# Three score banks and three side banks in twelve attention passes, with some additions on VectorE

## The chip, the cores and the metric

One core of one Trainium2 chip runs the whole kernel. The metric is the device time of one execution in microseconds (us). TensorE is called PE in the rows of the profile, VectorE DVE, ScalarE ACT, GpSimd POOL, and SyncE, which issues the DMAs here, SP.

## What is computed

The reference takes 1250 tokens of width 512 and does three things to them: a mean over neighbours in a graph with two linear layers, a linear attention, and then a block with two routed experts, a cross attention and an MLP. The part that matters here is the last block's attention, done three times with 8 heads of 64 features (spatial expert, temporal expert, cross attention):

```python
def _temporal_experts(xt, idx, qw, qb, kw, kb, vw, vb, pw, pb):
    q, k, v = ...                      # linear layers of xt, (B, T, H, HD)
    logits = jnp.einsum('bthd,bshd->bhts', q, k) * HD ** (-0.5)
    causal = jnp.tril(jnp.ones((T, T), dtype=bool))
    logits = jnp.where(causal, logits, -jnp.inf)
    att = jax.nn.softmax(logits, axis=-1)
    o = jnp.einsum('bhts,bshd->bthd', att, v).reshape(B, T, D)
    o = jnp.einsum('btd,bod->bto', o, pw[idx]) + pb[idx][:, None, :]
    return xt + o
```

The spatial one and the cross attention are the same without the causal mask. Products run in float32, most of them as three products of rounded parts (hi and lo).

## The kernel before

**Passes, units, steps.** The three attentions are 12 passes of two heads each: n = 0 to 3 spatial, 4 to 7 temporal with the causal mask, 8 to 11 cross. "The eighth pass" is n = 7 and "the last" is n = 11. A pass has five units, each 250 query tokens (i = 0 to 4), and a unit has five blocks of 250 keys (b), or i + 1 blocks where the mask is on. A step g is one head of one block; there are 520, so 260 pairs of steps. `STEP[g]` is (n, i, b, h).

**What a step does.** PE computes the scores of 250 keys and 250 queries into one bank of PSUM (`score`, L2357 to L2361; a bank holds 512 float32 in each partition, and there are eight). ACT takes the exponential of the bank into a ring of eight tiles, `p_raw` (`exponent`, L1380). For each pair of steps POOL adds the two heads' exponentials into `p_sum` (`add_pair`, L1085 to L1090: one instruction of 500 columns for a unit's first block, two for each later one). PE multiplies the exponentials by the values (`product`, L2376, a block of two pairs at a time), and at the end of a unit it multiplies `p_sum` by ones, which gives the denominators (`denominator`, L2386). DVE takes the reciprocal and multiplies (`unit_out`, L1817 and L1819).

**Side work.** Between the steps PE prepares what comes later, at most three side tasks a step (`SIDE[g]`): linear layers for keys, queries and values (K, Q, V: L2260), score products from which DVE takes the largest score of each query (M: `maximum`, L2318 on PE, L1801 on DVE), the turn of these maxima into a row (R: L2329 on PE, `row_in`, L1352 on ACT), the turn of the values (T: L2339) and the weights' product for the cross attention (F: L2299). A K leaves its bank when ACT has rounded it (`key_hi`, L1297) and DVE has taken the rest (`key_lo`, L1772); a Q likewise (`query_hi` L1325, `query_lo` L1783). `key_copy` (L1305) then copies each head's keys to the other half of the partitions, in two instructions of ACT.

**Banks.** Scores use banks 0 and 1 in turn (`g % 2`), the sums of a unit banks 2 and 3 (`unit % 2`), and side work the banks from `SIDE_BANKS_AT` = 4 on. `bank_plan` walks PE's list of work and gives each side task the side bank that was taken longest ago (one held by a K, Q or F of the same step is left out); `BEFORE[entry]` is what held the bank, and PE waits for that to be read (`left`). So with two score banks the scores of step g + 2 wait for the exponential of step g.

**Order.** All engines run a list that is written out in Python. On PE, slot g is: the scores of step g + 2 (`LEAD` = 2), `SIDE[g]`, then, at every second pair, denominators and products. On ACT, slot g is: the exponential of g + 2, the copies of `SIDE[g - 1]`, then the first readings of `SIDE[g]`. On DVE: `key_lo` and `query_lo` of `SIDE[g - 1]`, the maxima of `SIDE[g]`, `unit_out`; in the last five slots of the last pass also ten normalizations of `tok_z` (L1893), two a slot. On POOL: the pair's additions, then splits of weights (L952, L954) and of the finished attention planes (L1044, L1046). Between n = 7 and n = 8 PE projects the temporal result (`project`, L2397), and after n = 11 the cross result (`proj`, L2443); both need the last unit's output.

## Time and profile before

| | |
|---|---|
| median of 3 runs | 1836.44 us (1834.28 to 1839.62) |
| the profiled execution's own time | 1838.64 us |
| its span from first to last instruction | 1836.6 us |
| PE busy | 1652.5 us (90%) |
| DVE busy | 1066.6 us (58%) |
| ACT busy | 711.8 us (39%) |
| POOL busy | 875.5 us (48%) |
| attention steps, first to last score | about 467 to 1545 us |

The terms of a sum are made on the profiled execution. PE is the engine to follow: between the ends of the graph part and of the attention it is hardly ever idle, and all other engines feed it or read from it. Matmuls are pipelined and overlap in the rows, so the distance from start to start tells more than the busy time: a product of 250 columns starts 0.12 us after the one before it when nothing is in its way.

### The profile page before, as it was taken

What the parts mean: (1) busy time and instruction counts of PE and PEld (TensorE: products, weight loads), DVE (VectorE), ACT (ScalarE), POOL (GpSimd) and SP (SyncE); (2) the same over time, 40 slices, a digit from 0 to 9 for tenths busy, and PEclk for the clock granted to TensorE, in tenths of its full rate; (3) what the DMA queues carried; (4) which work ended last, traced back from release to release, by engine and by line L of the source; (5) the groups of instructions that cost most, each with busy time, mean ns of one, the idle gap of its engine ahead of it and who ended that gap; (6) DMA issues with size and microseconds to landing.
All of it is one profiled execution on the core that took longest, in us unless ns stands there. A gap on an engine that the chain in (4) does not pass through costs nothing. (4 is left out here: it accounts for less than half of the span.)

```text
span 1836.6 us, 32041 instructions
## 1 busy us (share of the span) xinstructions
PE 1652.5 (90%) x10735; PEld 1378.3 (75%) x10735; DVE 1066.6 (58%) x2221; ACT 711.8 (39%) x1346; POOL 875.5 (48%) x815
## 2 busy tenths in 40 slices
PE   2899988876899999999999997899999996899998
PEld 1788757755777888778878876788788874797896
DVE  7778768885556445654564562665555555683332
ACT  1223211114666445556555552464546553120010
POOL 3213001102587657684644466156566689383440
PEclk9999999988999999999999998899999998999999
DMA  3101000011031100030000000000000002121111
GB/s 116 35 7 47 12 1 29 18 49 50 12 125 41 35 19 7 1 130 12 18 13 7 7 1 24 17 19 7 7 13 13 1 1 85 40 74 35 46 35 56
DMA packets 24788, 58.06 MB, mean 32 GB/s; under 512 B 2537, under 2 KB 4805, under 8 KB 24013
## 3 DMA queue, kind: packets, MB, share of 16 engines
q1 hardware_dynamic: 24650, 56.18, 9.5%
q8 instruction: 92, 1.51, 0.3%
q14 instruction: 46, 0.38, 0.1%
HBM read 44.87 MB, written 11.30 MB: 31 GB/s over the span
## 5 line engine op out<-in xcount | busy, mean ns | idle before, releaser
L1801 DVE TENSOR_REDUCE max_part<-ps 125x2 f32<-125x500 f32 x520 | 328.1, 674 | 224.9 <-PE ps L2318 199.9
L1380 ACT ACTIVATE p_raw<-ps 125x500 f32<-125x500 f32 x520 | 296.9, 586 | 280.7 <-PE ps L2361 271.8
L1088 POOL TENSOR_TENSOR p_sum<-p_sum,p_raw 125x500 f32<-125x500 f32 x200 | 232.5, 1163 | 222.9 <-ACT p_raw L1380 215.7
L2376 PE MATMUL ps<-p_raw,v_rows 125*64 125x250 f32 x2080 | 248.5, 380 | 0.0
L1090 POOL TENSOR_TENSOR p_sum<-p_sum,p_raw 125x500 f32<-125x500 f32 x200 | 232.5, 1163 | 15.7
L2376 PEld LDWEIGHTS ps<-p_raw,v_rows 125*64 125x64 f32 x2080 | 143.4, 137 | 73.5 <-issue 4.5
L1641 DVE TENSOR_SCALAR onehot<-iota_h,win_key,key_t 125x320 f16 x453 | 176.9, 390 | 0.5 <-issue 0.4
L1817 DVE RECIPROCAL feat<-ps 128x250 f32<-128x250 f32 x60 | 103.0, 1717 | 113.8 <-PE ps L2386 113.6
L2260 PE MATMUL ps<-xa_hi,w_hi 128*128 128x418 f32 (+1 forms) x448 | 150.1, 335 | 14.5 <-POOL w_lo L954 9.1
L2357 PE MATMUL ps<-q_both_a,k_both_a 128*125 128x250 f32 x520 | 154.3, 317 | 9.4 <-ACT p_raw L1380 7.6
L2318 PE MATMUL ps<-k_both_a,q_both_a 128*125 128x250 f32 x520 | 143.8, 292 | 20.6 <-issue 9.1
L1640 DVE TENSOR_SCALAR onehot<-iota_h,low_t 125x125 f16 x453 | 128.2, 283 | 47.4 <-issue 26.5
L2357 PE MATMUL ps<-q_both_b,k_both_b 128*125 128x250 f32 x520 | 141.9, 294 | 12.9 <-ACT p_raw L1380 12.8
L2260 PE MATMUL ps<-xa_lo,w_hi 128*128 128x418 f32 (+1 forms) x448 | 148.3, 331 | 0.0
L2260 PE MATMUL ps<-xa_hi,w_lo 128*128 128x418 f32 (+1 forms) x448 | 148.0, 330 | 0.0
L2357 PEld LDWEIGHTS ps<-q_both_a,k_both_a 128*125 128x125 f32 x520 | 98.2, 189 | 65.5 <-issue 50.2
L2318 PE MATMUL ps<-k_both_b,q_both_b 128*125 128x250 f32 x520 | 140.5, 285 | 0.0
L2361 PE MATMUL ps<-q_row_a,k_rest_a 65*125 65x250 f32 x520 | 139.3, 289 | 0.0
L2361 PE MATMUL ps<-q_row_b,k_rest_b 128*125 128x250 f32 x520 | 137.8, 287 | 0.0
L2318 PEld LDWEIGHTS ps<-k_both_a,q_both_a 128*125 128x125 f32 x520 | 97.5, 188 | 27.7 <-issue 11.3
L952 POOL CAST w_hi<-w_raw 128x512 fp32r<-128x512 f32 x44 | 28.4, 645 | 183.4 <-PE ps L2361 48.2
L2357 PEld LDWEIGHTS ps<-q_both_b,k_both_b 128*125 128x125 f32 x520 | 98.2, 189 | 18.9 <-ACT p_raw L1380 18.6
(395 smaller groups left out, 3723.0 us busy)
## 6 DMA issues: line engine op xcount, KB each, us to landing
w_raw<-in_w_mlp SPq DMA_DIRECT2D x32, 256.0 KB, 2.7
w_raw<-in_w_gps SPq DMA_DIRECT2D x16, 256.0 KB, 2.6
w_raw<-in_w_tp SPq DMA_DIRECT2D x16, 256.0 KB, 2.6
w_raw<-in_w_sp SPq DMA_DIRECT2D x12, 256.0 KB, 2.7
w_raw<-in_w_cr SPq DMA_DIRECT2D x12, 256.0 KB, 2.6
d_xt<-xb_hi SPq DMA_DIRECT2D x1, 2508.0 KB, 9.4
d_xt<-xb_lo SPq DMA_DIRECT2D x1, 2508.0 KB, 15.0
xa_hi<-d_xt SPq DMA_DIRECT2D x1, 2508.0 KB, 9.3
```

The source lines that it names most:

```text
L1088: pool.tensor_tensor(total, total, halves[0], ALU.add).then_inc(s_add, 1)
L1090: pool.tensor_tensor(total, total, halves[1], ALU.add).then_inc(s_add, 1)
L1380: act.activation(p_raw[:, g % PR, :], ps[0:TOK, g % 2, 0:4 * TOK], ACT.Exp, scale=SCALE).then_inc(s_exp, 1)
L1640: dve.tensor_scalar(row[:, 0:ET], iota_h[0:ET, 0:ET], low, None, ALU.is_equal)
L1641: ins = dve.tensor_scalar(row[:, ET:ET + DH], iota_h[0:ET, :], win_key[0:ET, bass.ds(w, 1)], key, ALU.add, ALU.is_equal)
L1801: dve.tensor_reduce(part[:, y, :, j], ps[0:TOK, bank, 0:4 * TOK].rearrange("p (h k) -> p h k", h=2), AX.X, ALU.max)\
L1817: dve.reciprocal(out, ps[:, 2 + u % 2, 2 * TOK:4 * TOK]).then_inc(s_share, 1)
L2260: ins = pe.matmul(ps[:, bank, 0:width], w[:, ROLE_SLOT[role], 128 * c:128 * c + 128], x[:, c, first:first + width], start=(c == 0 and y == ...
L2318: ins = pe.matmul(to, q_both[h][:, ring(n, i), tile], k_both[h][:, n % 2, keys], start=True, stop=not masked)
L2357: pe.matmul(to, k_both[h][:, n % 2, tile], q_both[h][:, ring(n, i), :], start=True, stop=False)
L2361: ins = pe.matmul(to, k_rest[h][rest, n % 2, tile], q_row[h][rest, ring(n, i), :], start=False, stop=True)
L2376: ins = pe.matmul(ps[r, bank, 0:2 * TOK], v_rows[:, n % 2, kt, h, :], p_raw[:, (g - 1 + h) % PR, cols], start=(b == 0 and x == 0), stop=last)
```

## The change

Scores get three banks, 0 to 2 (`g % SCORE_BANKS`), the sums of a unit move to banks 3 and 4 (`OUT_BANK`), and side work keeps banks 5 to 7. In passes 7 and 11 (`SHARED`) POOL adds only the first head of each pair, in instructions of 250 columns, and DVE adds the second (`add_second_head`), at the head of its slot and behind a wait for that step's exponential; a semaphore of its own, `s_add_b`, tells PE's denominators and ACT's ring of these. `key_copy` is split: one head's copy in the slot after the K, as before, the other's one slot later (`third_out`), so the semaphore counts to six a pass.

```diff
-SIDE_BANKS_AT = 4
+SCORE_BANKS = 3
+OUT_BANK = 3
+SIDE_BANKS_AT = 5
...
+SHARED = (7, 11)
+SHARED_NO = {(n, i, b): 2 * x + 2 - (5 * y + i + 1) for y, n in enumerate(SHARED) for x, (m, i, b) in
+             [(x, at) for x, at in enumerate(at for at in ADDED if at[0] in SHARED) if at[0] == n]}
...
         if kind == "S":
-            use = [entry[1] % 2]
+            use = [entry[1] % SCORE_BANKS]
...
-            use = [2 + unit_of(entry[1]) % 2] if STEP[entry[1]][2] == 0 else []
+            use = [OUT_BANK + unit_of(entry[1]) % 2] if STEP[entry[1]][2] == 0 else []
...
-                total = p_sum[:, u % 2, :, :]
-                halves = [p_raw[:, (g - 1) % PR:(g - 1) % PR + 2, 2 * TOK * x:2 * TOK * (x + 1)] for x in range(2)]
-                pool.wait_ge(s_exp, g + 1)
+                heads = 1 if n in SHARED else 2
+                total = p_sum[:, u % 2, 0:heads, :]
+                halves = [p_raw[:, (g - 1) % PR:(g - 1) % PR + heads, 2 * TOK * x:2 * TOK * (x + 1)] for x in range(2)]
+                pool.wait_ge(s_exp, g - 1 + heads)
...
-                for h, r in enumerate(HALF):
-                    ins = act.activation(k_both[h][HALF[1 - h], n % 2, cols], f32(k_both[h][r, n % 2, cols]), ACT.Copy)
-                ins.then_inc(s_k_both, 1)
+                act.activation(k_both[h][HALF[1 - h], n % 2, cols], f32(k_both[h][HALF[h], n % 2, cols]), ACT.Copy).then_inc(s_k_both, 1)
...
                     act.wait_ge(s_add, ADD_NO[n, i, b])
+                    if n in SHARED:
+                        act.wait_ge(s_add_b, SHARED_NO[n, i, b])
...
+                    if g > first + 1:
+                        for task in SIDE[g - 2]:
+                            third_out(task)
...
+            def add_second_head(g):
+
+                n, i, b, _ = STEP[g]
+                u, done = 5 * n + i, SHARED_NO[n, i, b]
+                total = p_sum[:, u % 2, 1, :]
+                halves = [p_raw[:, g % PR, 2 * TOK * x:2 * TOK * (x + 1)] for x in range(2)]
+                dve.wait_ge(s_exp, g + 1)
+                if b == 0:
+                    dve.wait_ge(s_den, u - 1)
+                    dve.tensor_tensor(total, halves[0], halves[1], ALU.add).then_inc(s_add_b, 1)
+                else:
+                    dve.wait_ge(s_add_b, done - 2)
+                    dve.tensor_tensor(total, total, halves[0], ALU.add).then_inc(s_add_b, 1)
+                    dve.wait_ge(s_add_b, done - 1)
+                    dve.tensor_tensor(total, total, halves[1], ALU.add).then_inc(s_add_b, 1)
...
                 for g in range(first, end):
+                    if STEP[g][0] in SHARED and STEP[g][3] == 1:
+                        add_second_head(g)
...
-                pe.wait_ge(s_k_both, 3 * n + 3)
+                pe.wait_ge(s_k_both, 6 * n + 6)
...
                 pe.wait_ge(s_add, ADD_NO[n, i, blocks_in(n, i) - 1])
+                if n in SHARED:
+                    pe.wait_ge(s_add_b, SHARED_NO[n, i, blocks_in(n, i) - 1])
```

PE's instructions keep their order; what changes is what they wait for. In pass 5, at slot 232, stand the turned maxima of unit 2 (L2329), two score products for the maxima of unit 3 (L2318), the scores of step 235 (L2357), and in slot 233 the queries of unit 4 (L2260). Before:

```order
5535 L2329 MATMUL ps<-ident,max_col 33x125 [waits s_max_col,s_max_part]
5536 L2329 MATMUL ps<-ident,max_col 33x125
5537 L2318 MATMUL ps<-k_both_a,q_both_a 125x250 [waits s_k_both,s_q_lo,s_max_part]
5538 L2318 MATMUL ps<-k_both_b,q_both_b 125x250
5539 L2318 MATMUL ps<-k_both_a,q_both_a 125x250 [waits s_k_both,s_q_lo,s_max_part]
5540 L2320 MATMUL ps<-causal_mask,identb 125x250
5541 L2318 MATMUL ps<-k_both_b,q_both_b 125x250
...
5549 L2260 MATMUL ps<-xa_hi,w_hi 128x250 [waits s_w_split,s_k_lo]
```

The same place of the changed kernel, where the line numbers are 34 higher:

```order
5535 L2363 MATMUL ps<-ident,max_col 33x125 [waits s_max_col,s_max_part]
5536 L2363 MATMUL ps<-ident,max_col 33x125
5537 L2352 MATMUL ps<-k_both_a,q_both_a 125x250 [waits s_k_both,s_q_lo,s_max_part]
5538 L2352 MATMUL ps<-k_both_b,q_both_b 125x250
5539 L2352 MATMUL ps<-k_both_a,q_both_a 125x250 [waits s_k_both,s_q_lo,s_k_lo]
5540 L2354 MATMUL ps<-causal_mask,identb 125x250
5541 L2352 MATMUL ps<-k_both_b,q_both_b 125x250
...
5549 L2294 MATMUL ps<-xa_hi,w_hi 128x250 [waits s_w_split,s_max_in]
```

The wait for DVE's rest of the keys (`s_k_lo`) has moved from the Q in row 5549 to the second maximum in row 5539, two side tasks earlier, and the Q now waits for ACT's reading of the row that was turned in row 5535 (`s_max_in`).

ACT in the same slots: the readings of the K of pass 6 (L1297), the copies (L1305), the maxima's row (L1352), exponentials (L1380) and the first reading of the Q (L1325). Before:

```order
580 L1380 ACTIVATE p_raw<-ps 125x500
581 L1297 ACTIVATE k_both_a<-ps,tp_vecs 64x418
582 L1297 ACTIVATE k_both_b<-ps,tp_vecs 64x418
583 L1380 ACTIVATE p_raw<-ps 125x500
584 L1305 ACTIVATE k_both_a<-k_both_a 64x418
585 L1305 ACTIVATE k_both_b<-k_both_b 64x418
586 L1352 ACTIVATE q_row_a<-ps 1x250
587 L1352 ACTIVATE q_row_b<-ps 1x250
588 L1380 ACTIVATE p_raw<-ps 125x500
589 L1325 ACTIVATE q_both_a<-ps,tp_vecs 64x250
```

The changed kernel:

```order
587 L1387 ACTIVATE p_raw<-ps 125x500
588 L1304 ACTIVATE k_both_a<-ps,tp_vecs 64x418
589 L1304 ACTIVATE k_both_b<-ps,tp_vecs 64x418
590 L1387 ACTIVATE p_raw<-ps 125x500
591 L1311 ACTIVATE k_both_a<-k_both_a 64x418
592 L1357 ACTIVATE q_row_a<-ps 1x250
593 L1357 ACTIVATE q_row_b<-ps 1x250
594 L1387 ACTIVATE p_raw<-ps 125x500
595 L1311 ACTIVATE k_both_b<-k_both_b 64x418
596 L1330 ACTIVATE q_both_a<-ps,tp_vecs 64x250
```

The second copy has moved behind the row and the next exponential.

DVE at the end of the last pass, from the output of the last unit but one (L1817, L1819) to the rest of the attention planes (L1900). Before:

```order
1602 L1817 RECIPROCAL feat<-ps 128x250
1603 L1819 TENSOR_TENSOR feat<-ps,feat 128x250
1604 L1893 TENSOR_SCALAR tok_z<-tok_z,ln_mv,ln_r 125x512 x8
1605 L1817 RECIPROCAL feat<-ps 128x250
1606 L1819 TENSOR_TENSOR feat<-ps,feat 128x250
1607 L1893 TENSOR_SCALAR tok_z<-tok_z,ln_mv,ln_r 125x512 x2
1608 L1900 TENSOR_TENSOR oc_lo<-feat,oc_hi 128x418 x3
```

The changed kernel, with the unit's additions of the second head (L1838 to L1843) between them:

```order
1674 L1838 TENSOR_TENSOR p_sum<-p_raw 125x250
1675 L1841 TENSOR_TENSOR p_sum<-p_sum,p_raw 125x250
1676 L1843 TENSOR_TENSOR p_sum<-p_sum,p_raw 125x250
...
1679 L1849 RECIPROCAL feat<-ps 128x250
1680 L1851 TENSOR_TENSOR feat<-ps,feat 128x250
1681 L1927 TENSOR_SCALAR tok_z<-tok_z,ln_mv,ln_r 125x512 x4
1682 L1841 TENSOR_TENSOR p_sum<-p_sum,p_raw 125x250
1683 L1843 TENSOR_TENSOR p_sum<-p_sum,p_raw 125x250
1684 L1927 TENSOR_SCALAR tok_z<-tok_z,ln_mv,ln_r 125x512 x4
1685 L1841 TENSOR_TENSOR p_sum<-p_sum,p_raw 125x250
1686 L1843 TENSOR_TENSOR p_sum<-p_sum,p_raw 125x250
1687 L1849 RECIPROCAL feat<-ps 128x250
```

The last denominators now need additions (rows 1685 and 1686) that stand behind all eight of the first normalizations.

## Rows read from the trace of the kernel before

**Rows 1.** Waits: engine, line, what it waited for: us in total, times, longest.
```profile
PEld ps L2357 <- ACT p_raw L1380: 33.8, 62, 3.0
...
PE ps L2357 <- ACT p_raw L1380: 20.4, 46, 2.6
...
PE ps L2386 <- POOL p_sum L1090: 18.5, 3, 9.6
```
**Rows 2.** Timeline of PE, pass 9: start, us, engine, line, xcount, [idle before].
```profile
1321.18 0.44 PE L2357 MATMUL ps<-q_both_b,k_both_b 128*125 128x250 f32 x1 [1.79 <-ACT p_raw L1380]
```
**Rows 3.** Timeline of ACT at the same place.
```profile
1319.19 0.55 ACT L1305 ACTIVATE k_both_b<-k_both_b 64x418 fp32r<-64x418 f32 x1
```
**Rows 4.** Timeline of PE, pass 5: second maximum, queries, next unit's maxima.
```profile
939.95 0.28 PE L2318 MATMUL ps<-k_both_a,q_both_a 128*125 128x250 f32 x1
...
941.44 0.38 PE L2260 MATMUL ps<-xa_hi,w_hi 128*128 128x250 f32 x1 [0.20 <-DVE k_rest_b L1772]
...
943.88 0.28 PE L2318 MATMUL ps<-k_both_a,q_both_a 128*125 128x250 f32 x1
...
945.70 0.38 PE L2318 MATMUL ps<-k_both_a,q_both_a 128*125 128x250 f32 x1 [1.42 <-DVE q_both_b L1783]
```
**Rows 5.** Timeline of PE, pass 1: a maximum, two side tasks behind a turned row.
```profile
637.70 0.28 PE L2318 MATMUL ps<-k_both_a,q_both_a 128*125 128x250 f32 x1
```
**Rows 6.** Timeline of ACT at the same place: the row's reading.
```profile
637.74 0.37 ACT L1352 ACTIVATE q_row_b<-ps 1x250 fp32r<-1x250 f32 x1
```
**Rows 7.** Timeline of PE at the end of pass 7.
```profile
1127.45 1.10 PE L2386 MATMUL ps<-p_sum,ones_f 125*64 125x250 f32 x4 [9.61 <-POOL p_sum L1090]
```
**Rows 8.** Stretches: busy us and (xcount) by engine, granted clock, DMA share, GB/s.
```profile
1129.00:1133.00 4.00, 4.00 (x13) 3.81 (x12) 3.34 (x5) 1.44 (x3) 0.00 (x0) 0.50 0.00 0
1135.00:1139.00 4.00, 4.00 (x23) 3.95 (x22) 0.00 (x0) 0.00 (x0) 0.00 (x0) 1.00 0.00 0
1524.00:1529.00 5.00, 3.77 (x18) 2.18 (x20) 2.14 (x2) 0.00 (x0) 4.82 (x6) 0.50 0.32 134
```
**Rows 9.** Groups of POOL, 1088 to 1128 us: busy, mean ns | idle before.
```profile
L1088 POOL TENSOR_TENSOR p_sum<-p_sum,p_raw 125x500 f32<-125x500 f32 x9 | 10.4, 1158 | 0.3
...
L1046 POOL TENSOR_TENSOR k_rest_b<-feat,k_rest_a 128x418 fp32r<-128x418 f32 x3 | 2.8, 927 | 0.2
```
**Rows 10.** Groups of DVE, 1066 to 1098 us: the maxima.
```profile
L1801 DVE TENSOR_REDUCE max_part<-ps 125x2 f32<-125x500 f32 x24 | 15.4, 675 | 4.7 <-PE ps L2318 2.9 <-PE ps L2320 1.5
```
**Rows 11.** Groups of DVE, 1472 to 1520 us: the maxima.
```profile
L1801 DVE TENSOR_REDUCE max_part<-ps 125x2 f32<-125x500 f32 x31 | 19.8, 675 | 16.6 <-PE ps L2318 16.4
```
**Rows 12.** Timeline of PE at the end of pass 11.
```profile
1525.22 1.10 PE L2386 MATMUL ps<-p_sum,ones_f 125*64 125x250 f32 x4 [4.53 <-POOL p_sum L1090]
...
1551.43 1.10 PE L2386 MATMUL ps<-p_sum,ones_f 125*64 125x250 f32 x4 [4.36 <-POOL p_sum L1090]
1560.21 0.76 PE L2443 MATMUL ps<-wout_hi,oc_hi 128*125 128x512 f32 x1 [7.68 <-DVE oc_lo L1900]
```
**Rows 13.** Timeline of DVE, end of pass 11; last row: beside an idle POOL.
```profile
1544.23 0.42 DVE L1819 TENSOR_TENSOR feat<-ps,feat 128x250 f32<-128x250 f32 x1
1544.56 9.91 DVE L1893 TENSOR_SCALAR tok_z<-tok_z,ln_mv,ln_r 125x512 f32<-125x512 f32 x8
1554.39 1.71 DVE L1817 RECIPROCAL feat<-ps 128x250 f32<-128x250 f32 x1
...
1578.32 1.92 DVE L1942 TENSOR_SCALAR tok_z<-tok_x,end_mv,end_r 125x512 f32<-125x512 f32 x4
```
**Rows 14.** Timeline of POOL after pass 7.
```profile
1143.13 0.61 POOL L952 CAST w_hi<-w_raw 128x512 fp32r<-128x512 f32 x1 [15.73 <-PE ps L2397]
...
1145.06 1.85 POOL L952 CAST w_hi<-w_raw 128x512 fp32r<-128x512 f32 x1
```
**Rows 15.** Timeline of DVE beside the second of these.
```profile
1144.66 1.78 DVE L1830 TENSOR_TENSOR feat<-feat,xa_lo 128x1254 f32<-128x1254 f32 x1
```

More of the change, by code:

```diff
@@ L717, in build @@
         s_add = sem("s_add")
+        s_add_b = sem("s_add_b")
         s_den = sem("s_den")
@@ L1298, in key_hi, with key_copy @@
                 ins.then_inc(s_k_hi, 1)
-            def key_copy(n, p):
+            def key_copy(n, p, h):
                 cols = slice(NP * p, NP * p + NP)
                 act.wait_ge(s_k_hi, 3 * n + p + 1)
-                for h, r in enumerate(HALF):
-                    ins = act.activation(k_both[h][HALF[1 - h], n % 2, cols], f32(k_both[h][r, n % 2, cols]), ACT.Copy)
-                ins.then_inc(s_k_both, 1)
+                act.activation(k_both[h][HALF[1 - h], n % 2, cols], f32(k_both[h][HALF[h], n % 2, cols]), ACT.Copy).then_inc(s_k_both, 1)
             def query_bias(n):
@@ L1379, in exponent @@
                     act.wait_ge(s_add, ADD_NO[n, i, b])
-                act.activation(p_raw[:, g % PR, :], ps[0:TOK, g % 2, 0:4 * TOK], ACT.Exp, scale=SCALE).then_inc(s_exp, 1)
+                    if n in SHARED:
+                        act.wait_ge(s_add_b, SHARED_NO[n, i, b])
+                act.activation(p_raw[:, g % PR, :], ps[0:TOK, g % SCORE_BANKS, 0:4 * TOK], ACT.Exp, scale=SCALE).then_inc(s_exp, 1)
             def first_out(task):
@@ L1401, in second_out, with third_out @@
                 if what == "K":
-                    key_copy(*at)
+                    key_copy(*at, 0)
                 if what == "Q":
                     query_copy(*at)
+            def third_out(task):
+                what, *at = task
+                if what == "K":
+                    key_copy(*at, 1)
             act.wait_ge(s_ld_ev, 32)
@@ L1426, in _ @@
                 query_hi(n, 0)
-                key_copy(n, 0)
-                key_copy(n, 1)
-                key_copy(n, 2)
+                for p in range(3):
+                    for h in range(2):
+                        key_copy(n, p, h)
                 value_feat(n, 0)
@@ L1816, in unit_out @@
                 dve.wait_ge(s_den, u + 1)
-                dve.reciprocal(out, ps[:, 2 + u % 2, 2 * TOK:4 * TOK]).then_inc(s_share, 1)
+                dve.reciprocal(out, ps[:, OUT_BANK + u % 2, 2 * TOK:4 * TOK]).then_inc(s_share, 1)
                 dve.wait_ge(s_share, u + 1)
-                dve.tensor_tensor(out, ps[:, 2 + u % 2, 0:2 * TOK], out, ALU.mult).then_inc(s_o, 1)
+                dve.tensor_tensor(out, ps[:, OUT_BANK + u % 2, 0:2 * TOK], out, ALU.mult).then_inc(s_o, 1)
             def project(j, cols, done):
@@ L2355, in score @@
                     tile = slice((2 * b + x) * TOK, (2 * b + x + 1) * TOK)
-                    to = ps[0:TOK, g % 2, 2 * TOK * x:2 * TOK * (x + 1)]
+                    to = ps[0:TOK, g % SCORE_BANKS, 2 * TOK * x:2 * TOK * (x + 1)]
                     pe.matmul(to, k_both[h][:, n % 2, tile], q_both[h][:, ring(n, i), :], start=True, stop=False)
@@ L2366, in product @@
                 n, i, b, _ = STEP[g]
-                bank = 2 + unit_of(g) % 2
+                bank = OUT_BANK + unit_of(g) % 2
                 pe.wait_ge(s_exp, g + 1)
@@ L2382, in denominator @@
                 n, i = u // 5, u % 5
-                bank = 2 + u % 2
+                bank = OUT_BANK + u % 2
                 pe.wait_ge(s_add, ADD_NO[n, i, blocks_in(n, i) - 1])
+                if n in SHARED:
+                    pe.wait_ge(s_add_b, SHARED_NO[n, i, blocks_in(n, i) - 1])
                 for h, r in enumerate(HALF):
```

## The prediction, made before the changed kernel ran

> **What bounds the kernel now.** I read the waits of the attention first, then the timelines at the places that they name. PE is the engine to follow. Its waits there are of three kinds. Many short ones are scores that wait for an exponential [rows 1]: by the weight loads 33.8 us in 62 places, by the matmuls 20.4 us in 46. The second kind is three denominators that wait for POOL's additions, 18.5 us [rows 1]: 9.61 us at the end of the eighth pass [rows 7], 4.53 and 4.36 us at the end of the last [rows 12]. The third kind is side work that waits for DVE or ACT to read its bank or to finish an operand, as the maximum behind the queries' rest [rows 4]. So there is no single bound engine to relieve: PE would run through if three small supplies were a little earlier, and the change speeds up two of them and takes a bank from the third.
>
> **The change part by part.** All terms are for the profiled execution, 1838.64 us, which lies 2.2 us above the median of 1836.44.
>
> *Three banks for scores.* The scores of step g + 2 now need the exponential of g - 1, not of g. That exponential ends a whole step earlier, and a step with its side work is longer than nearly every wait seen: the longest is 3.0 us [rows 1]. The sample place shows why: in pass 9 scores waited 1.79 us [rows 2], because ACT stood in two key copies of 0.55 us, the second of them [rows 3], and in a row's reading before the exponential. With three banks that exponential isn't on the path of these scores. The weight loads' sum of 33.8 us overlaps work that is still running, the matmuls' sum of 20.4 us leaves out the restart; from the distances of starts in the timeline I get about 30. I take -28, with bounds of -20 and -33. The split key copy brings an exponential 0.55 us forward where a row or an exponential stands behind it, and puts the other head's copy one slot later, where its readers are at least a slot away. With three banks little is left for it to gain: 0, bounds -2 and +3.
>
> *Three banks for side work.* Now a side task waits for the reader of the task three back instead of four. I walked the new owners along the times of before. Five patterns come out. (a) The second maximum behind a K waits for the keys' rest. In pass 5 it starts at 939.95 and the rest is ready at about 941.4, when the Q started that waited for it [rows 4]: +1.5. The next maximum at 943.88 then waits for the queries' rest, which came at 945.6 [rows 4] and was waited for anyway, so a part is only moved: 1.3 net, at about 5 places, 6.5 us. (b) A maximum behind a turned row waits for its reading: in pass 1 the maximum starts at 637.70 [rows 5], the reading began at 637.74 and took 0.37 [rows 6], so about 0.4 plus a restart of 0.1, less a quarter of a microsecond of wait that it replaces: 0.26 at 22 places, 5.7 us. (c) A linear layer whose bank a query or key holds: at most the size of that wait for the queries' rest, 1.42 [rows 4], in the mean 1.07, at 8 places: 8.5 us. (d) Bursts of maxima: DVE takes 675 ns for one [rows 10], PE four products of 0.12 us, and one bank less means that the burst is felt one task earlier: 0.45 at 20 places, 9 us. (e) A few single keys and maxima, 4 us. The sum is +34. The upper bound is what all new latenesses add up to if none is absorbed by another, +69, of which half is not to be believed, since a late task makes its successors late too; I take 55. If later waits absorb most of it, 15 is left. I take 34, since I followed each pass with its shifts.
>
> *Denominators of the eighth pass.* POOL has no gap from 1088 us to the wait's end: idle before its additions is 0.3 us, an instruction of 500 columns takes 1158 ns, one of 418 columns 927 [rows 9]. By proportion 250 columns take 0.58 and by the line through both 0.45; I take 0.6, for the fixed part. That is 0.55 saved in each of some 20 instructions, 11 us, more than the 9.61 [rows 7]; the wait goes, what is next is the last exponential, so I count -9.5. Behind the wait PE's granted clock was 0.50: 13 matmuls in 4 us, 23 in 4 us when it was 1.00 again [rows 8]. From 1127.5 until 1133.6, where it changed, that lost 6.1 x (1 - 13/23), some 2.7 us. Without the idle time I count them back: -12.2 in all, bounds -4 and -13.
>
> *Denominators of the last pass.* The same relief comes to the first wait of 4.53 [rows 12], with the halved clock after it [rows 8] worth 2 us more: -6.5, bounds -3 and -7. At the last wait of 4.36 [rows 12] it is not the same. The additions of the second head stand on DVE behind normalizations that took 9.91 us for eight, 1.24 us each beside a busy POOL; beside an idle one the same form takes 0.48 [rows 13]. If POOL is half idle, eight take about 7 us; the four additions that now stand before the last denominators add 1.6 to 3. In the old order the reciprocal had to wait behind the eight anyway, until 1554.39 [rows 13]. So the end of that DVE chain, which the projection waits for (7.68 us [rows 12]), moves by little: -1.5, bounds -5 and +3. The three denominators together: **-20**, bounds -10 and -25.
>
> *VectorE's additions.* No row shows such an instruction. A product of 250 columns with an operand in PSUM took 0.42 [rows 13]; if it has to take turns with POOL's halved addition, the 0.6 of above comes on top. So 0.4 to 1.0 each. In the stretch of pass 7 that I looked at, DVE's idle time before the 24 maxima is 4.7 us [rows 10], and some 7 pairs come in, 14 additions of 0.4 or more, 5.6 us at least. That doesn't fit, so the maxima come later there and their banks with them: +3, bounds 0 and +8. In pass 11 the idle time is 16.6 us in 48 [rows 11] and some 32 additions want 13 us and up: +4, bounds 0 and +14. Each addition waits for its exponential at the slot's head, and the queries' rest and the maxima are queued behind it; this is in those bounds. Together +7.
>
> The sum: -28 + 34 - 20 + 7 = -7. 1838.6 - 7 = 1831.6, less 2.2 for the median: **1829.4**.
>
> **The rivals.** *(1) Side banks become the bound.* If a step's three side tasks do not absorb each other's lateness, the side term is 47, and with DVE short of time in the passes 7 and 11 the additions cost 9: -27 + 47 - 18 + 9 = +11, so 1847. It decides from a side term of about 45 on. For it speaks that three supplies (keys' rest, queries' rest, turned row) each show at least one wait with four banks already [rows 4]; against it that most of these are waits for an operand, which are there with any number of banks.
>
> *(2) The additions take turns.* POOL's CAST of 512 columns took 0.61 us when alone, and 1.85 us when DVE ran an addition with both inputs in SBUF [rows 14], from 1144.66 on for 1.78 us [rows 15]: it ended when DVE's did and its own 0.6 were over. If POOL's halved additions stand still while DVE's run, they take 0.6 + 0.4 = 1.0 instead of 1.16, 3 us are saved of 9.61, the clock stays low behind the rest, and the terms are -4 at pass 7, -6.5 at pass 11, and +8 for DVE: -28 + 34 - 10.5 + 8 = +3.5, so 1840. Against it: in that row the DVE instruction was long, and short ones may fall beside each other.
>
> The Trainium skill, "SBUF — State Buffer", section "Who interferes with whom", makes a law of it: a VectorE instruction with two SBUF inputs contends with a GpSimd instruction that reads SBUF, and whoever is second stands still for the whole instruction. By that rule rival 2 is the case for every pair in which the two meet. The two rows of the CAST agree with it.
>
> *(3) The side banks hardly matter.* Waits for operands remain the later ones, and the side term is 18: -29 + 18 - 20 + 5 = -26, so 1810. For it: the wait of pass 5 shows how a new wait eats an old one [rows 4]. Against it: the walk has this in it already.
>
> *(4) The third score bank doesn't do what it says.* If ACT is behind by more than a step where scores waited, half of the 28 stays, and the sum is +7: 1843. Against it: the longest wait is 3.0 us [rows 1], and a step takes PE more than that with its side work.
>
> **How the numbers follow.** Forecast 1829, own range 1820 to 1837: 0.42. Rival 1: 0.17. Rival 2: 0.15. Rival 3: 0.18. Rival 4: 0.08. What a measurement of this kernel can tell from no change is about 0.3%, 5.5 us: faster is below 1830.9, slower above 1841.9. Of the forecast 0.26 lies below and 0.16 within; rival 3 is all faster; rival 2 gives 0.02 faster, 0.09 within and 0.04 slower; rival 1 gives 0.03 within and 0.14 slower; rival 4 gives 0.01, 0.03 and 0.04. That makes faster 0.47, within 0.31, slower 0.22. The range, 1811 to 1847, leaves out half of rival 1 and half of rival 3, under 0.2.
>
> **What would show it.** Right: no waits of scores for exponentials but a few; the wait before the denominators of pass 7 under 1 us, and granted clock 1.00 in the projection behind it; waits of side work for ACT's row and DVE's rests and maxima up by some 30 us; POOL's halved additions at 0.6 us and DVE's at about 0.4; the last reciprocal within 3 us of its old distance to the last scores. Wrong: POOL's halved additions near 1.0 us (rival 2), side waits of 45 us or more (rival 1), or scores that still wait for ACT (rival 4). The forecast would fail first in the side term, which is the largest and comes from a walk, not from a row.

## The result, and the profile of the changed kernel

| | before | changed |
|---|---|---|
| median | 1837.03 us (4 runs) | 1848.88 us (4 runs, 1848.59 to 1850.63) |
| span of the profiled execution | 1836.6 us | 1847.0 us |
| ratio | | 1.0063, 95% interval 1.0051 to 1.0075 |

The changed kernel is slower by 11.8 us where 7 us less were forecast. The waits of the whole trace come first: engine, line (34 higher than before for PE), what it waited for, us in total, times, longest. First those of the changed kernel:

```profile
PEld ps L2352 <- DVE max_part L1817: 15.7, 27, 2.3
PEld ps L2352 <- DVE q_both_b L1799: 14.1, 14, 1.9
...
PEld ps L2352 <- ACT q_row_b L1357: 11.6, 17, 2.2
...
PEld ps L2352 <- DVE k_rest_b L1788: 10.1, 9, 1.5
...
PE ps L2422 <- DVE p_sum L1843: 11.8, 1, 11.8
...
PE ps L2422 <- POOL p_sum L1097: 4.8, 1, 4.8
...
PEld ps L2391 <- ACT p_raw L1387: 2.6, 7, 0.4
```

The rows of before that answer to the first three (nothing there answers to the fourth: no maximum waited for the keys' rest):

```profile
PEld ps L2318 <- ACT q_row_b L1352: 8.0, 15, 1.8
PEld ps L2318 <- DVE q_both_b L1783: 7.7, 6, 1.6
...
PEld ps L2318 <- DVE max_part L1801: 0.6, 2, 0.3
```

Scores hardly wait any more: 2.6 us of weight loads where [rows 1] has 33.8. Side work waits far more, most of all score products for a bank whose last maximum DVE hasn't read yet: 0.6 us before, 15.7 now. And the denominators, three waits and 18.5 us in [rows 1], are now two waits and 16.6 us: one of them is longer than any was, and its releaser has changed from POOL to DVE.

At the end of the last pass the forecast had the wrong path. PE, then DVE, then POOL of the changed kernel (start, us, engine, line, xcount, idle before):

```profile
1565.67 1.10 PE L2422 MATMUL ps<-p_sum,ones_f 125*64 125x250 f32 x4 [11.80 <-DVE p_sum L1843]
1570.54 0.76 PE L2479 MATMUL ps<-wout_hi,oc_hi 128*125 128x512 f32 x1 [3.77 <-DVE oc_lo L1934]
```
```profile
1551.70 2.62 DVE L1927 TENSOR_SCALAR tok_z<-tok_z,ln_mv,ln_r 125x512 f32<-125x512 f32 x4
1554.25 1.47 DVE L1841 TENSOR_TENSOR p_sum<-p_sum,p_raw 125x250 f32<-125x250 f32 x1
1555.75 1.36 DVE L1843 TENSOR_TENSOR p_sum<-p_sum,p_raw 125x250 f32<-125x250 f32 x1
1557.04 5.69 DVE L1927 TENSOR_SCALAR tok_z<-tok_z,ln_mv,ln_r 125x512 f32<-125x512 f32 x4
1562.65 1.47 DVE L1841 TENSOR_TENSOR p_sum<-p_sum,p_raw 125x250 f32<-125x250 f32 x1
1564.15 1.36 DVE L1843 TENSOR_TENSOR p_sum<-p_sum,p_raw 125x250 f32<-125x250 f32 x1
1566.80 1.72 DVE L1849 RECIPROCAL feat<-ps 128x250 f32<-128x250 f32 x1 [1.28 <-PE ps L2422]
```
```profile
1553.35 0.69 POOL L1097 TENSOR_TENSOR p_sum<-p_sum,p_raw 125x250 f32<-125x250 f32 x1
1554.00 11.24 POOL L1122 TENSOR_TENSOR tok_z<-tok_z,bias_out 125x512 f32<-125x512 f32 x8
```

POOL is done with its additions at 1554.0 and goes straight on to its next work, the bias additions to `tok_z`, 1.4 us each. In the very same stretch DVE's four additions take 1.36 to 1.47 us instead of 0.42, and a normalization takes 1.42 (5.69 for four) instead of 0.65 (2.62 for four, before 1554). The chain from 1551.70 to 1565.5 is all DVE's, and PE stands at its end, idle for 11.80 us. The rows of before that answer to these are [rows 12] and [rows 13], and POOL's next work stood in that trace too, right behind its last addition of 500 columns:

```profile
1551.34 14.28 POOL L1115 TENSOR_TENSOR tok_z<-tok_z,bias_out 125x512 f32<-125x512 f32 x10
```

The wait itself overstates the loss. The reciprocal no longer stands behind the normalizations, so the wait of the projection behind it falls from 7.68 [rows 12] to 3.77. From the start of the last score product (L2357, now L2391) to the start of the projection it is 15.4 us before and 18.9 us now: 3.5 us lost at this place.

### The profile page after: what moved, and what is told of

Its sections match the earlier page's. It is cut to its first block, busy times and chain, and to the rows that moved or that the text cites. A ratio compares the mean times of both kernels' runs of the same rounds, so it can differ in the third digit from the quotient of the medians.

```text
span 1847.0 us, 32232 instructions
## 1 busy us (share of the span) xinstructions
PE 1656.4 (90%) x10735; PEld 1380.2 (75%) x10735; DVE 1109.6 (60%) x2291; ACT 709.2 (38%) x1346; POOL 850.5 (46%) x815
## 4 chain that ended last, share of the span: by engine, by line
PE 72%; DVE 12%; issue 5%; ACT 3%; POOL 2%; DVEq 2%; DMA 2%; SPq 0%; ACTq 0%; POOLq 0%
PE ps L2294 14%; PE ps L2410 11%; PE ps L2479 8%; PE ps L2391 6%; PE ps L2352 5%; PE ps L2078 5%; PE ps L2395 5%; PE ps L2508 5%; DVE max_part L1817 2%; PE ps L2215 2%; PE ps L2433 2%; PE ps L2422 2%; PE ps L2091 2%; DMA tok_a<-in_x 1%; DVE onehot L1656 1%
## 5 line engine op out<-in xcount | busy, mean ns | idle before, releaser
L1817 DVE TENSOR_REDUCE max_part<-ps 125x2 f32<-125x500 f32 x520 | 329.7, 675 | 212.2 <-PE ps L2352 182.5
L1095 POOL TENSOR_TENSOR p_sum<-p_sum,p_raw 125x500 f32<-125x500 f32 (+1 forms) x200 | 221.5, 1108 | 229.3 <-ACT p_raw L1387 222.8
L1097 POOL TENSOR_TENSOR p_sum<-p_sum,p_raw 125x500 f32<-125x500 f32 (+1 forms) x200 | 217.9, 1090 | 15.7
L2352 PE MATMUL ps<-k_both_a,q_both_a 128*125 128x250 f32 x520 | 149.8, 303 | 45.3 <-DVE q_both_b L1799 11.4
L2391 PE MATMUL ps<-q_both_a,k_both_a 128*125 128x250 f32 x520 | 151.5, 311 | 3.0 <-issue 3.0
L2352 PEld LDWEIGHTS ps<-k_both_a,q_both_a 128*125 128x125 f32 x520 | 97.5, 188 | 61.1 <-DVE max_part L1817 15.7
L2391 PE MATMUL ps<-q_both_b,k_both_b 128*125 128x250 f32 x520 | 139.6, 289 | 0.0
L2391 PEld LDWEIGHTS ps<-q_both_a,k_both_a 128*125 128x125 f32 x520 | 98.2, 189 | 52.7 <-issue 50.0
L2215 PE MATMUL ps<-onehot 125*125 x453 | 87.6, 311 | 24.2 <-DVE onehot L1657 24.0
```

The costliest lines, as they stand in the source:

```text
L1095: pool.tensor_tensor(total, total, halves[0], ALU.add).then_inc(s_add, 1)
L1097: pool.tensor_tensor(total, total, halves[1], ALU.add).then_inc(s_add, 1)
L1817: dve.tensor_reduce(part[:, y, :, j], ps[0:TOK, bank, 0:4 * TOK].rearrange("p (h k) -> p h k", h=2), AX.X, ALU.max)\
L2352: ins = pe.matmul(to, q_both[h][:, ring(n, i), tile], k_both[h][:, n % 2, keys], start=True, stop=not masked)
L2391: pe.matmul(to, k_both[h][:, n % 2, tile], q_both[h][:, ring(n, i), :], start=True, stop=False)
```

## The experiments

Each kernel was timed beside the kernel before, on one chip; ratios are to that. There are three such groups: `e_banks`, `e_side3`, `e_share` and `e_late`; `e_pool_wait`, `e_share_late`, `e_best` and `e_before_late`; `e_tiny` and `e_nosplit`. The changed kernel's 1848.88 us is from a fourth. The kernel before came out at 1837.03, 1838.34, 1838.24 and 1838.79 us in the four, so a difference to a kernel of another group is uncertain by about 2 us; where it matters, both figures are given, of the medians as they stand and of each against its own before.

All these kernels give PE the same 10735 matmuls in the same order. So the distance from one start to the next can be compared, matmul by matmul, between two traces, and the sum of the differences says where the time went.

**Which half loses: banks or additions?** `e_banks` is the change of banks alone:

```diff
-SHARED = (7, 11)
+SHARED = ()
...
                 if what == "K":
                     key_copy(*at, 0)
+                    key_copy(*at, 1)
...
-                    if g > first + 1:
-                        for task in SIDE[g - 2]:
-                            third_out(task)
```

> Only the banks change (three for scores, three for side work); POOL adds both heads everywhere and the key copies stay together. Theory A (the banks alone make the loss: stalls of scores -29 us, stalls of side work more than +40): 1847 to 1853 us, with about 17 us lost between the first scores of pass 0 and of pass 7. Theory B (the banks cost the 6 us of my walk, the rest is lost by the additions on VectorE): 1840 to 1844 us, at most 10 us lost before pass 7. Both: the three waits of denominators stay near 9.6, 4.5 and 4.4 us.

Measured: 1851.65 us against 1838.34, ratio 1.0068 (1.0051 to 1.0085), 13.3 lost. The trace is 17.2 us behind at the first scores of pass 7, and passes 9 to 11 win a part back. The banks alone lose all that the change loses, as theory A has it. By the distances, scores take 33.9 us less and side work 42.0 more. Its waits:

```profile
PE ps L2420 <- POOL p_sum L1097: 25.1, 5, 10.7
...
ACT p_raw L1387 <- POOL p_sum L1097: 10.8, 7, 3.2
```

The waits of denominators were to stay and did not: 25.1 us where [rows 1] has 18.5. In the passes 7 and 11 PE, freed of its waits for exponentials, arrives earlier at denominators for which POOL is not done, and ACT waits for POOL too, 10.8 us, to get a tile of its ring back. What the third score bank gains in pass 7, POOL takes back: the pass takes 123.6 us here, 123.4 in `e_side3` below, which has two score banks.

`e_side3` has two banks for scores and three for side work; bank 4 is unused:

```diff
-SCORE_BANKS = 3
-OUT_BANK = 3
+SCORE_BANKS = 2
+OUT_BANK = 2
 SIDE_BANKS_AT = 5
-SHARED = (7, 11)
+SHARED = ()
```

(and the key copies together, as above.)

> Two banks for scores as before, but three for side work (one of the eight is left unused). Measures the price of the fourth side bank by itself. Theory A: waits of scores stay near 28 us, side stalls rise from 41 to 70 us or more, time 1862 to 1872 us. Theory B: the side term is the 34 us or less of the walk and part of it hides under the scores' own waits: 1850 to 1862 us. If side waits only move what the scores waited for anyway: within 5 us of before.

Measured: 1876.47 us, ratio 1.0200 (1.0183 to 1.0217). With two banks for scores the fourth side bank is worth 38.1 us, above every theory's number; with three for side work the third score bank is worth, by difference to `e_banks`, 24.8. Where the 38 are, by its waits:

```profile
PEld ps L2350 <- DVE q_both_b L1797: 12.6, 10, 1.9
...
PEld ps L2350 <- ACT q_row_b L1357: 10.3, 17, 2.1
PEld ps L2350 <- DVE max_part L1815: 10.3, 19, 2.3
PEld ps L2350 <- DVE k_rest_b L1786: 10.1, 9, 1.5
```

By the distances from start to start, all of it is in the side work: 39.8 us more between the first scores and the cross projection, 25.8 in front of products for maxima, 15.6 in front of linear layers and 1.6 less in front of the rest, while scores take 2.6 less. The idle time that PE's rows show in front of these matmuls grows by only 22.2 us; the other 17.6 are in distances that grew while the rows show PE busy. So the waits of PE's rows undercount such stalls.

The clock is a rival for a part of it. In pass 4, before and here (columns as in [rows 8], the granted clock is the number behind POOL's), it fell:

```profile
853.00:925.00 72.00, 67.82 (x519) 58.47 (x518) 38.72 (x61) 40.48 (x81) 38.91 (x38) 1.00 0.04 12
```
```profile
868.00:945.00 77.00, 70.68 (x524) 59.84 (x523) 39.00 (x61) 40.81 (x81) 39.37 (x38) 0.98 0.04 11
```

A stretch that ran at 1.00 throughout now runs at 0.98 in the mean, which is 1.5 us of 77. But over the whole execution the mean granted clock is 0.965 in both traces: (1 - 0.9647) x 1836.6 = 64.8 us before and (1 - 0.9645) x 1874.7 = 66.5 us here. So the clock can account for some 2 of the 38 us at most; what pass 4 lost by it, other stretches gave back.

`e_share` is the additions alone, with the banks and copies of before:

```diff
-SCORE_BANKS = 3
-OUT_BANK = 3
-SIDE_BANKS_AT = 5
+SCORE_BANKS = 2
+OUT_BANK = 2
+SIDE_BANKS_AT = 4
 SHARED = (7, 11)
```

> Banks and copies as before; only the second head's additions go to VectorE in passes 7 and 11. Theory A: the gain at pass 7's denominators (4 to 9 us with the clock) and at the last unit but one (6 us) stands against 8 us lost at the last denominators: 1829 to 1836 us. Theory B: 1840 us or more, since the additions hold up the maxima too. Both: VectorE's additions 0.42 us where POOL does nothing, 0.65 to 0.85 beside POOL's.

Measured: 1831.10 us, ratio 0.9958 (0.9941 to 0.9975), 7.2 saved. Theory A is right again. PE at the end of pass 7, and at the end of pass 11:

```profile
1121.16 0.64 PE L2420 MATMUL ps<-p_sum,ones_f 125*64 125x250 f32 x4 [2.19 <-POOL p_sum L1097]
...
1547.06 1.10 PE L2420 MATMUL ps<-p_sum,ones_f 125*64 125x250 f32 x4 [11.49 <-DVE p_sum L1841]
```

With the banks of before the wait in pass 7 falls from 9.61 [rows 7] to 2.19. From the first scores of pass 7 to those of pass 8 it saves 10.0 us, where the forecast had 12.2 less 3. The last wait is 11.49 us here as well, so it has nothing to do with the banks. In front of the side work of pass 11 the distances grow by 3.2 us, in that of pass 7 by 0.5: this is what DVE's additions cost the maxima, with four side banks.

**Why the last wait grew.** `e_late` is the changed kernel with the normalizations moved:

```diff
-                    if g in XN_AT:
-                        dve.wait_ge(s_xn_back, 16)
-                        for t in XN_AT[g]:
-                            dve.tensor_scalar(tok_z[:, t, :], ...).then_inc(s_xn, 1)
...
+            def normal(t):
...
+            dve.wait_ge(s_xn_back, 16)
+            normal(0)
+            normal(1)
             for p in range(3):
                 dve.wait_ge(s_oc_hi, p + 1)
...
+            for t in range(2, 6):
+                normal(t)
...
                 ins = dve.bn_stats(end_stats[:, t, :], tok_x[:, t, :])
...
+                if t < 4:
+                    normal(t + 6)
```

> The changed kernel, with the ten normalizations of tok_z on VectorE moved from the last five slots of the last pass to behind the last unit's output (two before the rests of the attention planes, the others behind and between the sums). Theory A (the normalizations ahead of the last additions, slowed by POOL's bias additions that start as soon as they can, make the last wait of 12 us): that wait falls under 3 us and the time by 8 to 11 us, to 1838 to 1841. Rival (the wait is made by the additions alone, which take turns with POOL): it falls by 8.3 us of normalizations less what the projection then waits for, 1843 to 1846. If the projection waits for the late normalizations: no gain, 1848.

Measured: 1840.44 us (10 runs), ratio 1.0008 (0.9998 to 1.0017), 8.4 less than the changed kernel's 1848.88, or 9.8 with each against its own before. Theory A: the last wait falls to 0.43 us, and from the last scores to the projection it is 8.2 us instead of 18.9. But the moved normalizations are not free. From the projection to the end of the kernel this trace takes 280.0 us, that of the changed kernel 276.4; of the 3.6 us, 2.0 are a wait of PE for DVE before it turns the next normalized tokens. DVE's last additions in it:

```profile
1549.07 0.70 DVE L1841 TENSOR_TENSOR p_sum<-p_sum,p_raw 125x250 f32<-125x250 f32 x1
1549.81 0.73 DVE L1843 TENSOR_TENSOR p_sum<-p_sum,p_raw 125x250 f32<-125x250 f32 x1
1551.36 1.72 DVE L1849 RECIPROCAL feat<-ps 128x250 f32<-128x250 f32 x1 [0.83 <-PE ps L2429]
```

`e_pool_wait` leaves the order alone and takes POOL away instead:

```diff
             pool.wait_ge(s_ld_bias, 16)
+            pool.wait_ge(s_den, 60)
             for t in range(NT):
                 pool.wait_ge(s_xn, t + 1)
                 pool.tensor_tensor(tok_z[:, t, :], tok_z[:, t, :], bias_out[:, :], ALU.add).then_inc(s_resid, 1)
```

> The changed kernel with one edit: POOL's bias additions to tok_z (which began at 1554.00 us in its trace, beside VectorE's last additions) wait until the last denominators are done. Contention theory: VectorE's last four additions take 0.42 us instead of 1.36 to 1.47, four of its normalizations 0.65 instead of 1.42, so the last wait falls from 12 to 5 us and the time by 5 to 7, to 1842 to 1844. Rival (VectorE's order alone sets it, POOL's part is small): the wait stays above 9 us, 1847 or more. If the projection then waits for the late bias additions, the wait falls but the time doesn't.

Measured: 1843.25 us (10 runs), ratio 1.0029 (1.0018 to 1.0040), 5.6 less than the changed kernel (6.8 with each against its own before). DVE's chain and PE's wait, now without POOL beside it:

```profile
1553.43 0.41 DVE L1842 TENSOR_TENSOR p_sum<-p_sum,p_raw 125x250 f32<-125x250 f32 x1
1553.87 0.42 DVE L1844 TENSOR_TENSOR p_sum<-p_sum,p_raw 125x250 f32<-125x250 f32 x1
1554.20 1.91 DVE L1928 TENSOR_SCALAR tok_z<-tok_z,ln_mv,ln_r 125x512 f32<-125x512 f32 x4
```
```profile
1557.04 0.64 PE L2423 MATMUL ps<-p_sum,ones_f 125*64 125x250 f32 x4 [4.03 <-DVE p_sum L1844]
```

The same instructions in the same order: 0.42 instead of 1.4 us for an addition, 0.48 instead of 1.42 for a normalization. Of the wait of 11.80 POOL's bias additions make 7.8, the order on DVE the other 4. A part of the 7.8 is paid behind it, as the kernel's expectation allowed: PE's wait before the projection is 6.0 us instead of 3.77.

**Do the two engines take turns?** `e_tiny` is the changed kernel with the additions on DVE cut to 2 columns; the rest of the second head's sums is left out.

```diff
-                    dve.tensor_tensor(total, total, halves[0], ALU.add).then_inc(s_add_b, 1)
+                    dve.tensor_tensor(total[:, 0:2], total[:, 0:2], halves[0][:, 0:2], ALU.add).then_inc(s_add_b, 1)
```

(the other two likewise)

> The changed kernel, but VectorE's additions of the second head are done on 2 of the 250 columns only (the other columns of the second head's sums are left out, so these denominators are stale); order and semaphores stay. It takes VectorE's share away from POOL's. If the two engines take turns: POOL's additions of 250 columns fall from 0.79, 0.68 and 0.70 us to 0.62 all of them, the wait before the denominators of pass 7 falls from 5.0 to 1 or 2 us, the last wait from 12 to 6 or 7 (the eight normalizations stay), and with the side work's waits of passes 7 and 11 the time falls by 11 to 15 us, to 1834 to 1838. If they don't: POOL's stay near 0.73, pass 7's wait stays near 5 us, and the time falls by the last wait's 5 us alone, to 1843.

Measured: 1838.96 us (10 runs), ratio 1.0001 (0.9991 to 1.0011), 9.9 less than the changed kernel, or 11.7 with each against its own before: "turns", whose range was 11 to 15. Its details came out less well: the wait of pass 7 is 2.7 us, not 1 or 2, and the last wait 12.0, not 6 or 7. The groups of POOL's halved additions in the whole trace (busy, mean ns | idle before), in the changed kernel and then in `e_tiny`:

```profile
L1095 POOL TENSOR_TENSOR p_sum<-p_sum,p_raw 125x250 f32<-125x250 f32 x30 | 23.7, 789 | 5.1 <-ACT p_raw L1387 3.9
L1097 POOL TENSOR_TENSOR p_sum<-p_sum,p_raw 125x250 f32<-125x250 f32 x30 | 20.3, 676 | 2.3
...
L1843 DVE TENSOR_TENSOR p_sum<-p_sum,p_raw 125x250 f32<-125x250 f32 x30 | 23.8, 795 | 1.0
```
```profile
L1095 POOL TENSOR_TENSOR p_sum<-p_sum,p_raw 125x250 f32<-125x250 f32 x30 | 21.6, 720 | 6.1 <-ACT p_raw L1387 5.1
L1097 POOL TENSOR_TENSOR p_sum<-p_sum,p_raw 125x250 f32<-125x250 f32 x30 | 18.9, 629 | 2.3
```

The second row falls to what was expected, the first only to 0.72. And DVE's two-column additions of `e_tiny`, one pair before POOL's bias additions began at 1546.04, one beside them:

```profile
1539.17 0.31 DVE L1841 TENSOR_TENSOR p_sum<-p_sum,p_raw 125x2 f32<-125x2 f32 x1 [2.41 <-ACT p_raw L1387]
1539.51 0.16 DVE L1843 TENSOR_TENSOR p_sum<-p_sum,p_raw 125x2 f32<-125x2 f32 x1
...
1546.07 1.25 DVE L1841 TENSOR_TENSOR p_sum<-p_sum,p_raw 125x2 f32<-125x2 f32 x1
1547.35 1.18 DVE L1843 TENSOR_TENSOR p_sum<-p_sum,p_raw 125x2 f32<-125x2 f32 x1
```

These are the clearest rows of the study. An addition of 2 columns takes 0.16 us in a gap between two of POOL's instructions and 1.2 us beside POOL's bias additions, which take 1.3 us each in this trace: it waits for one to end. Even the 0.31 fits: that addition ended at 1539.48, and POOL's own, which had begun at 1538.74 and took 0.72, at 1539.46. So an addition on DVE costs what POOL is doing at that moment, not what its own size says. The Trainium skill, "SBUF — State Buffer", section "Who interferes with whom", says that a VectorE instruction with two SBUF inputs and a GpSimd one that reads SBUF exclude one another for a whole instruction; these rows agree.

The last wait did not fall here, against the expectation. PE's last scores come 4.1 us earlier with respect to the pass's start, while DVE's chain gets little shorter: its last four additions, though of 2 columns, still take 4.8 us beside POOL instead of 5.7, and the eight normalizations 8.0 instead of 8.3. That their size hardly matters is the same finding once more.

**Is it additive, and is there a better kernel?** `e_share_late` is `e_share` with the normalizations moved as in `e_late`; `e_before_late` moves them in the kernel before; `e_best` is `e_share_late` with the key copies over two slots (`third_out`).

> Banks and copies of before, the second head's additions on VectorE in passes 7 and 11, and the ten normalizations behind the last unit's output. If the last wait (11.7 us in the run with shared additions alone) is VectorE's order, it falls below 1 us and the time to 1821 to 1824 us, 8 below that run, as it did with the changed kernel's banks (8.4 less). If not additive, 1828 to 1831.

Measured: 1823.53 us against 1838.24, ratio 0.9928 (0.9910 to 0.9946): within its range, 7.6 less than `e_share`, so the two changes add up as expected.

> As e_share_late, with the key copies split over two slots: with two score banks an exponential that stands behind a copy comes 0.55 us earlier. If these are on the path of the scores' waits (28 us in all, some 46 of them): 2 to 5 us less than e_share_late. If the later second copy holds up the maxima as much: the same within 1 us.

Measured: 1819.52 us (1818.84 to 1820.08), ratio 0.9900 (0.9883 to 0.9916), another 4.0 saved. The scores' waits, of `e_share_late` and of `e_best`:

```profile
PEld ps L2396 <- ACT p_raw L1387: 33.6, 61, 3.0
```
```profile
PEld ps L2398 <- ACT p_raw L1387: 25.8, 58, 1.3
```

The longest wait falls from 3.0 to 1.3 us: those were exponentials behind key copies. This kernel beats the one before by 18.7 us and the changed one by 29 to 31. It too takes 3.5 us more behind the projection than the changed kernel (279.9 against 276.4), so a better place for the late normalizations may be worth up to that; this was not run.

> The kernel before with the ten normalizations behind the last unit's output, nothing else. POOL's additions end the last pass there (wait of 4.4 us), and VectorE's last reciprocal waits 2 us behind the normalizations. Expected: the wait of 4.4 stays or shrinks little (POOL runs without VectorE beside it), the reciprocal follows at once, 2 to 3 us less than before, 1834 to 1836. If the normalizations hid nothing else: no change.

Measured: 1838.84 us (10 runs), ratio 1.0001 (0.9991 to 1.0011). Moving the normalizations alone gives nothing in the time, but both parts of the expectation show in the trace. The last wait stays (4.14 us), since POOL makes it. The reciprocal does follow at once, and the projection starts 2.8 us sooner behind the last denominators, 5.95 instead of 8.78 us. Behind it the late normalizations take this back, 279.3 us to the end instead of 276.4:

```profile
1557.84 0.76 PE L2484 MATMUL ps<-wout_hi,oc_hi 128*125 128x512 f32 x1 [4.85 <-DVE oc_lo L1935]
...
1580.91 2.30 PE L2505 MATMUL ps<-ident,tok_z 125*128 125x125 f32 x10 [1.99 <-DVE tok_z L1981]
```

PE did not wait at this second place before. So in the kernel before the new place costs what the old one did, and the new order is worth something only where the normalizations hold up the last denominators.

**What does the split give beside three score banks?** `e_nosplit` is the changed kernel with the copies together.

> The changed kernel with both heads' keys copied in one slot, as before. With two score banks the split gave 4 us, at places where scores waited for an exponential behind a copy. With three score banks these waits are gone, so the split has nothing to give: the time stays at 1848.9 within 1.5. If the later second copy costs maxima: 1 to 3 us less than 1848.9.

Measured: 1847.79 us, ratio 1.0052 (1.0035 to 1.0070), 1.1 less than the changed kernel by the medians and 2.9 with each against its own before, with intervals of the ratios that overlap. The 4 us of `e_best` are not there with three score banks. Whether the split costs up to 3 us or nothing is open.

## Why the prediction was wrong, by its own steps

The step that failed is the term of the denominators, -20: they gave 5.5 us in the changed kernel, because POOL's relief did not reach the last denominators, where DVE's chain beside POOL's next work took its place, and reached those of pass 7 by half. The prediction's bounds for the three denominators together, -10 and -25, were also narrower than its own parts: -4, -3 and +3 add up to -4, and -5.5 lies inside that. The side work, put at +34 and +7, took 51.7 us and adds the rest of the miss. By medians:

| step | forecast | measured | by |
|---|---|---|---|
| three score banks | -28 | -24.8 | `e_banks` less `e_side3` |
| three side banks | +34 | +38.1 | `e_side3` |
| additions, all of it | -20 + 7 = -13 | -4.3 beside three side banks, -7.2 beside four | `e_nosplit` less `e_banks`, each to its own before; `e_share` |
| key copies split | 0 | +1.1 or +2.9, not resolved | `e_nosplit` |

And by PE's distances from start to start, from the first scores to the cross projection, as differences in us to the kernel before, all from the profiled executions:

| in front of | forecast | changed | `e_banks` | `e_side3` | `e_share` |
|---|---|---|---|---|---|
| scores | -28 | -34.3 | -33.9 | -2.6 | -0.3 |
| side work | +34 + 7 | +51.7 | +42.0 | +39.8 | +3.6 |
| denominators and the projections behind them | -20 | -5.5 | +5.2 | -0.8 | -11.7 |
| everything else | 0 | -1.8 | +0.2 | +1.5 | -0.3 |
| sum | -7 | +10.1 | +13.5 | +37.9 | -8.7 |

**The last denominators had the wrong path.** "If POOL is half idle, eight take about 7 us; the four additions that now stand before the last denominators add 1.6 to 3", so -1.5. They took 8.3 us, and the four additions 5.7. POOL was not half idle. I asked what POOL's relief frees, but not what POOL does next: its bias additions followed at once and stood beside exactly the instructions that were to gain. The wait went from 4.36 [rows 12] to 11.80, and with the shorter wait of the projection 3.5 us were lost where 1.5 were to be gained. Rival 2 had the mechanism and the row for it [rows 14, 15], but I applied it to the halved additions alone, where it costs little, and gave 1840. The first wait of the last pass came out as forecast: 4.6 us less in front of its denominators and 1.6 in the products behind them, of 6.5.

**Pass 7 was a term of the wrong size, and the largest part of the miss.** Forecast were -12.2 us; in the changed kernel the denominators gave 4.4 and the projection behind them nothing. In `e_share` the two gave 7.6 and 2.5, so with four side banks the term was near. The -4 that rival 2 gave for this pass is what came. Two things differ from the forecast. POOL's halved additions were put at 0.6 us; they take 0.79, 0.68 and 0.70 on average in the changed kernel (0.72, 0.63 and 0.63 in `e_tiny`, where DVE's are 2 columns wide). And pass 7 begins with stalls of side work: step 302 starts 30.2 us after the pass's first scores instead of 28.0 in `e_share`, POOL's run without a gap starts 2.2 us later, and the wait is 4.84 us where `e_share` has 2.19. The clock behind it stays low too, in the changed kernel:

```profile
1143.00:1147.00 4.00, 4.00 (x13) 3.81 (x12) 2.88 (x5) 1.43 (x3) 0.00 (x0) 0.50 0.00 0
```

13 matmuls in 4 us, just as in [rows 8]. The 2.7 us that I counted back for the clock did not come here: behind a wait of 4.84 us the granted clock was 0.50 for 6.8 us. In `e_pool_wait`, behind the same wait, it was 0.50 for only 3.4 us, and pass 7 took 116.9 us instead of 119.2, so a part of this varies from one execution to the next. Behind the waits of 2.19 us in `e_share` and 2.75 in `e_tiny` it stayed at 1.00, and there the 2.5 us came.

**Side banks: the walk was near, its "moved" waits were not.** The term was +34, and the side banks took 38.1 us by medians, 39.8 and 42.0 by the distances. The prediction gives its sum for all passes together, so the miss can't be placed by pass. In `e_banks` the passes 0 to 3 take +2.9, +3.3, -0.6 and -0.1 us in all, the passes 4 to 6 +4.4, +3.7 and +3.7: in these three the distances in front of scores change by 0.3 us at most, so nothing pays for the lost bank. Its pattern (a) said of pass 5 that the new wait for the keys' rest would shrink the next one for the queries' rest. The place in the changed kernel:

```profile
950.59 0.38 PE L2352 MATMUL ps<-k_both_a,q_both_a 128*125 128x250 f32 x1 [1.33 <-DVE k_rest_b L1788]
...
951.83 0.28 PE L2294 MATMUL ps<-xa_hi,w_hi 128*128 128x250 f32 x1
...
955.99 0.38 PE L2352 MATMUL ps<-k_both_a,q_both_a 128*125 128x250 f32 x1 [1.66 <-DVE q_both_b L1799]
```

The new wait is there, 1.33 us, but the next is 1.66 where [rows 4] has 1.42. The queries whose rest is waited for are computed between the two. From their start to the maximum that needs them it is 4.26 us in [rows 4], 941.44 to 945.70, and 4.16 here. The new wait delays the producer as well as the consumer, so nothing is absorbed. A late instruction hides in a later wait only if what that wait is for does not come after it.

**DVE's additions: right.** The +7 for the maxima that they hold up was 7.9 us by the distances (`e_nosplit` less `e_banks`: 0.9 in pass 7, 7.0 in pass 11).

**Scores: right in kind.** "no waits of scores for exponentials but a few" held: 2.6 us. By the distances scores took 34.3 us less, so -28 was even too little. But it took gains in passes whose end POOL sets, and `e_banks` gave 6.6 us of them back in the denominators' waits, 25.1 against 18.5. That conflict was in the sum: the wait of pass 7 was removed by one term and the gain in scores before it by another, and both can count only if POOL's relief is as large as forecast.

**Rival 1** came nearest in time, 1847, in part by luck. Its side work was near, 47 + 9 against 51.7, and its sign, side waits of 45 us or more, is there in the changed kernel. But its condition, a side term of about 45 from the banks, did not hold (38.1 to 42.0), and its -27 for scores and -18 for denominators were 7 and 12 us off in opposite directions. The forecast named the side term as the one that would fail first. It failed by 4 us, the denominators by 14.

## What to carry to other kernels

When a change relieves an engine, read what stands next in its queue and beside what on other engines it will then run: here POOL's next eight instructions added 7.8 us to a wait that had been 4.4 us in all. A wait that is moved ahead of the instruction that produces the next operand is not hidden by the wait for that operand. And where two resources compete for one pool, measure each side alone before the sum: the bank given was worth 25 us and the bank taken 38. When work is moved off a path, look for what waits for it at its new place: the moved normalizations gave some 3 us back behind the projection, which the time of `e_late` alone does not show.

## What the hardware showed that I had not expected

- An addition of 2 columns on VectorE with both inputs in SBUF took 0.16 us, and 1.2 us beside GpSimd's additions of 512 columns (`e_tiny`). A normalization of 512 columns with one input tile took 0.48 us alone and 1.42 beside them (`e_pool_wait` and the changed kernel).
- Idle time in PE's rows undercounts many short stalls: in `e_side3` side work took 39.8 us more by the distances from start to start, and the rows show 22.2 us more idle time in front of it.
- The granted clock stayed at 1.00 behind waits of 2.19 and 2.75 us (`e_share`, `e_tiny`) and was 0.50 behind one of 4.8 us, for 6.8 us in one execution and 3.4 in another with the same waits up to there.
